# Moving four of sixteen heads of a score product from GpSimd to VectorE, and a division one step later

## What is computed

```python
att = jnp.einsum('bthd,btgd->bthg', q, k) / jnp.sqrt(jnp.float32(Dh))   # Dh = 8
att = jax.nn.softmax(att, axis=-1)
out = jnp.einsum('bthg,btgd->bthd', att, v)
...
x = x + _L0_attn_ref(xn, ...) + _L0_ffn_ref(xn, ...)     # top 2 of 8 experts
```

## Time and profile before

| | |
|---|---|
| median of 3 runs | 1330.55 us (1329.0 to 1339.67) |
| the profiled execution's own time | 1335.22 us |
| its span, first to last instruction | 1333.3 us |
| busy: TensorE, weight loads, VectorE, ScalarE, GpSimd | 1042.1, 879.2, 739.9, 583.7, 803.9 us |
| GpSimd's products L294 | 42, 188.8 us |
| GpSimd's scatters of results L498, both layers | 284, 283.3 us |
| score reduces L1157 | 21, 92.6 us |

### The profile page before, as it was taken

One profiled execution on the slowest core, in us unless ns is written; L12 is line 12 of the kernel. 1 busy time (PEld: TensorE's weight loads), 2 busy tenths in 40 slices (PEclk: granted clock), 3 DMA queues, 4 the chain that ended last, 5 costly groups with the idle time before them and its releaser, 6 DMA issues. The chain is left out here.

```text
span 1333.3 us, 19064 instructions
## 1 busy us (share of the span) xinstructions
PE 1042.1 (78%) x6498; PEld 879.2 (66%) x6498; DVE 739.9 (55%) x953; ACT 583.7 (44%) x1518; POOL 803.9 (60%) x669
## 2 busy tenths in 40 slices
PE   5553776788988898888714678898879999999995
PEld 4521333367777777777613577888868888888884
DVE  7755988998888898888697643211122200000007
ACT  1200111166676777767503673000006666666651
POOL 4065675568888888888875136566544544444444
PEclk9876886799999999999856888998979999999998
DMA  9912322335554555555281021698966867666649
GB/s 294 355 47 102 120 84 109 108 93 151 155 162 139 154 170 149 161 150 159 68 325 57 1 84 44 197 279 252 296 196 195 270 193 196 194 190 196 199 135 356
DMA packets 120245, 226.03 MB, mean 170 GB/s; under 512 B 16961, under 2 KB 80405, under 8 KB 118102
## 3 DMA queue, kind: packets, MB, share of 16 engines
q1 hardware_dynamic: 102164, 188.45, 46.1%
q0 software_dynamic: 17600, 35.71, 7.3%
q10 hardware_dynamic: 386, 0.66, 0.2%
HBM read 157.33 MB, written 67.42 MB: 169 GB/s over the span
## 5 line engine op out<-in xcount | busy, mean ns | idle before, releaser
L498 POOL DMA_INDIRECT y_tok<-FF,yidx x284 | 283.3, 997 | 205.9 <-ACT FF L586 142.6
L490 POOL DMA_INDIRECT sorted_x<-XN,idx x256 | 247.9, 968 | 140.1 <-issue 88.0
L810 PE MATMUL ps<-FF 128*128 128x128 f32 x2272 | 285.8, 280 | 0.0
L810 PEld LDWEIGHTS ps<-FF 128*128 128x128 f32 x2272 | 274.0, 197 | 15.6 <-issue 4.8
L797 PE MATMUL ps<-FF 128*128 128x256 f32 x1136 | 272.3, 383 | 0.0
L576 ACT ACTIVATE FF<-ps,FF 128x256 f32<-128x256 f32 x568 | 231.4, 473 | 36.8 <-PE ps L797 29.1
L797 PEld LDWEIGHTS ps<-FF 128*128 128x128 f32 x1136 | 206.9, 192 | 22.7
L294 POOL TENSOR_TENSOR BG<-TPB 128x2048 f32<-128x2048 f32 x42 | 188.8, 4519 | 30.0 <-ACT TPB L603 20.8
L838 PE MATMUL ps<-BG,cst 128*128 128x512 f32 x176 | 105.4, 767 | 57.8 <-DVE BG L1144 40.5
L1176 DVE TENSOR_TENSOR BG<-ps,TPB 128x1024 f32<-128x1024 f32 x128 | 147.3, 1212 | 0.0
L1187 DVE TENSOR_REDUCE BG<-BG 128x256 f32<-128x4096 f32 x32 | 141.0, 4406 | 0.0
(11 more groups left out here) (203 smaller groups left out, 1462.0 us busy)
## 6 DMA issues: line engine op xcount, KB each, us to landing
FF<-in_moe SPq DMA_DIRECT2D x142, 514.0 KB
TPB<-in_kpad SPq DMA_DIRECT2D x22, 1024.0 KB
sorted_x<-TPB SPq DMA_DIRECT2D x36, 520.0 KB, 5.4
FF<-sorted_x SPq DMA_DIRECT2D x142, 130.0 KB
BG<-y_tok SPq DMA_DIRECT2D x12, 1024.0 KB, 9.2
FF<-in_kpad SPq DMA_DIRECT2D x10, 1024.0 KB
y_tok<-FF,yidx POOLq DMA_INDIRECT x284
xt_d<-BG SPq DMA_DIRECT2D x16, 256.0 KB, 4.4
```

Source lines behind the costliest of these rows:

```text
L490: pool.indirect_dma_start(sorted_x[layer], bass.IndirectOffsetOnAxis(ap=idx[:, k, j:j + 1], axis=0), XN[:, j, :], None).then_inc(s_sc, 16)
L498: pool.indirect_dma_start(y_d[layer], bass.IndirectOffsetOnAxis(ap=yidx[:, G % 4, r:r + 1], axis=0), ys[:, G % 4, r * D:(r + 1) * D], None ...
L810: t = pe.matmul(psY[:, r * P:(r + 1) * P], hT[:, G % 2, m, r * P:(r + 1) * P], wc[:, G % 4, HID + m * D:HID + (m + 1) * D], start=False, s ...
```

## The change

In `scores(b)`, for `b` from 10 to 30, VectorE waits until q, k and v of pair `b + 1` are copied, and multiplies the last four heads of the second tile of pair `b + 1`. This stands behind the score reduce of pair `b` and ahead of its maximum. GpSimd's second half of a product shrinks from 16 heads to 12. The score reduce waits for both. The division (`by_sums`, formerly the end of `weighted`) of pairs 10 to 29 moves from the end of step `b + 1` into step `b + 2`, behind the score reduce and behind the new product, ahead of the maximum. Other pairs keep it in its old place.

```diff
+H_DVE = 4
...
-                    for t in range(2):
-                        qk_product(pool, b + 1, t).then_inc(s_pp, 1)
+                    qk_product(pool, b + 1, 0).then_inc(s_pp, 1)
+                    qk_product(pool, b + 1, 1, 0, H - H_DVE).then_inc(s_pp, 1)
...
+            mine, divided = {}, {}
+
             def scores(b):
...
                     dve.wait_ge(s_pp, 2 * (b - OWN) + 2)
+                    dve.wait_ge(s_v, mine[b])
                     link(dve.tensor_reduce(S[:, b % 2, :], prod[:, b % 2, :].rearrange("p (n d) -> p n d", d=DH),
                                            AX.X, ALU.add))
                     raw = S3
+                if OWN - 1 <= b < NPAIR - 1:
+                    dve.wait_ge(s_qkv, 2 * (b + 1) + 2)
+                    mine[b + 1] = mark(qk_product(dve, b + 1, 1, H - H_DVE, H_DVE))
+                if b > OWN:
+                    by_sums(b - 2)
                 wait(dve, s_sub, b)
                 link(dve.tensor_reduce(Mx, raw, AX.X, ALU.max))
...
                 reduced = mark(dve.tensor_reduce(O, prodv.rearrange("p (n g) -> p n g", g=H), AX.X, ALU.add))
-                dve.wait_ge(s_v, max(inverted, reduced))
+                divided[b] = max(inverted, reduced)
+                if not OWN - 1 <= b < NPAIR - 2:
+                    by_sums(b)
+
+            def by_sums(b):
+
+                dve.wait_ge(s_v, divided[b])
                 wait(dve, s_ot, b - 2)
                 dve.tensor_tensor(On[:, b % 3, :].rearrange("p (n e) -> p n e", e=DH), O.rearrange("p (n e) -> p n e", e=DH),
                                   Rc[:, :, None].to_broadcast([P, 2 * H, DH]), ALU.mult).then_inc(s_on, 1)
```

## The result

The changed kernel takes 1342.30 us in the median of 20 runs (1329.71 to 1352.03), the kernel before 1329.40 us in 20 runs beside it (1321.49 to 1339.67). The ratio is 1.0089, with a 95% interval of 1.0069 to 1.0110: about 12 us slower, where 2 us were forecast. The profiled execution took 1343.59 us, with a span of 1341.6. In the changed file the lines have moved by 2 to 16: the product is L296, the scatter L500, the copy of q, k, v L605, ScalarE's work on a finished tile L586 and L588; VectorE's score reduce is L1162, maximum L1171, subtraction L1172, `add_heads` L1177, division L1206.

The account below looks back on a forecast made before the run. GpSimd's loop of products, scatters and a wait for ScalarE's copy was taken as the bound. Start +1.4, nine two-pair stretches at +0.2, end -1.1 gave about +2 on the median 1330.55: 1333 us, range 1314 to 1345.

Parts of the forecast that it names:

- the new wait: VectorE waits for the next pair's copy before the maximum; even products start 2.50 us behind it, 2.41 more than before.
- rival B: Ring of four result buffers rules, ScalarE waits for landed first scatters; two pairs grow 1.3 us, 1345 us; chance 0.13.
- the sum per two pairs: GpSimd's loop over two pairs: -2.2 from its shorter halves, +2.41 from the later even start, +0.2 us.
- GpSimd's second half: GpSimd's product with 12 heads in place of 16: 1.1 us saved a pair, 2.2 for two.
- VectorE's new product: VectorE's product of 512 elements ahead of the maximum: taken as 0.61 us, upper end 0.69.
- Odd pairs unchanged: GpSimd's odd products start as before, behind the eight scatters, with 1.25 us of cover left.
- Start of the stretch: Pairs 10 to 12: GpSimd's product of pair 12 starts at 292.2 in place of 290.85, +1.4 us.
- End of the stretch: From the product of pair 30 on, everything comes 1.1 us earlier relative to that product's start.
- The copy: ScalarE's copy of q, k, v before an even product was taken as tied to the end of GpSimd's six scatters.
- rival A: Copy not tied to the scatters' end, time falls: 1320 us, chance 0.16, or 1297 us, chance 0.07.
- The two never meet: VectorE's new product and GpSimd's product of the same pair never overlap, since GpSimd's waits for the subtraction.
- Rival C: GpSimd's second half stays near 4.5 us despite fewer heads: +23 us, 1354 us; chance 0.05.

Follow-up runs that it names:

- experiments 3: Kernel before plus only VectorE's wait for the next pair's q, k, v copies ahead of the maximum; 1342.03 us, ratio 1.0093.
- experiment 8: Changed kernel with the division put back into its old place, ahead of the score reduce; 1334.48 us, ratio 1.0057 to the kernel before.
- experiment 5: Kernel before with the two scatters of each step's first tile moved between the halves of GpSimd's product; 1318.35 us, ratio 0.9950.
- experiment 12: Kernel before with each step's last tile scattered between the halves of GpSimd's next product; 1324.28 us, ratio 0.9985.
- experiment 2: Changed kernel reduced to the moved division: GpSimd multiplies all 16 heads, VectorE none, no wait for the copy; 1327.28 us, ratio 0.9989.
- experiment 6: Kernel of experiment 1 with the two scatters of each step's first tile moved between GpSimd's product halves; 1308.99 us, ratio 0.9866.
- experiment 1: Changed kernel with VectorE's four heads multiplied one step later, just ahead of their own score reduce; 1330.49 us, ratio 1.0032.

## Why the prediction came out as it did

The forecast was no change that can be told, 1333 us; 1342 lies inside its range, and the ratio of 1.0089 just inside its bound of 1%. The loop, the new wait and its price were read rightly. That the time stayed inside the range is in part luck: its upper end stood where it did for rival B. The step that failed is the sum per two pairs, +0.2 us, which measured +1.61, so that the loss is six times the 2 us forecast. (A slip besides: by its own terms the forecast's inner range should begin at 1333 - 11 = 1322, not 1324.)

- *GpSimd's second half*, -2.2 per two pairs: -2.16. Right.
- *VectorE's new product*, 0.61 us: 484.50 to 485.11. Right.
- *The new wait*, even products 2.50 us behind the copy: 2.60. Right, and experiments 3 and 8 show its parts: 1.65 for the wait with maximum and subtraction, 0.34 for the division.
- *Odd pairs unchanged*: right.
- *Start of the stretch*, +1.4: right. From the end of pair 11's copy, for which the first of the new waits waits, to the start of product 12 it took 18.00 us before (272.85 to 290.85) and 19.51 now (271.68 to 291.19). Counted from the start of the span product 12 is only 0.34 later, because this execution came to pair 11's copy 1.17 us earlier:

```profile
271.20 0.48 ACT L605 COPY TPB<-ps 128x384 f32<-128x384 f32 x1 [1.67 <-PE ps L855]
291.19 7.92 POOL L296 TENSOR_TENSOR BG<-TPB 128x2048 f32<-128x2048 f32 x2 [9.31 <-DVE BG L1172]
```

- *End of the stretch*, -1.1: product 30 starts 14.8 us later than before and the last scatter of layer 0 ends 13.4 later (681.70 against 668.30): -1.4. Right. From pair 11's copy to that scatter the change costs 14.6 us. The two profiled executions end only 8.3 us apart: besides the 1.17 us at the start, 5 us were made up behind that scatter, which the change does not touch, and why isn't shown.
- *The copy*, taken as fixed to the end of the six scatters: it came 0.78 us later. This is the first term that was missing. It did stay behind the last scatter (rival A fell), but its distance isn't fixed, and under another order of the scatters it ends ahead of them (experiment 5). Why the distance grew stays open.
- *"The two never meet"*: true of the two products. But VectorE's product and subtraction met GpSimd's scatters, in the run of eight, and each stretched one: +0.65 there, +0.46 for both runs, the second missing term. Before, the subtraction did so only at times: the scatter at 514.40 took 1.45 us.

Rival B named a time near to the measured one, but its sign did not come: ScalarE's stop for landed scatters is 1.34 us at 498.70, against 1.04, and did not grow by the 1 us that the prediction asked of it. From 270 to 690 us ScalarE's waits ahead of a finished tile are now these (those of the kernel before stand under experiment 12):

```profile
ACT yidx L586 <- remote: 47.2, 18, 3.6
...
ACT yidx L586 <- DMA y_tok<-FF,yidx: 15.1, 10, 2.1
```

The waits for landed scatters grew from 11.7 to 15.1 us, those without a named releaser from 23.8 to 47.2. Still, the copy kept its distance to the first of the eight scatters better than that to the last of the six: 28.48 us before and 28.64 after on the mean of the nine, against 1.89 and 2.68. So B's sum, +1.3 per two pairs, is nearer to the +1.61 than the forecast's, without the cause that it named. Rival C fell with the halves. The division cost the 0.34 that the prediction gave it in the chain (experiment 8), and nothing by itself (experiment 2).

## What to carry to other kernels

Before an engine is given work ahead of a result that others wait for, look at when its inputs come: a wait in that place was paid in full here, and it ate the whole gain of a lighter GpSimd. If the input is late, ask first why; reordering GpSimd's scatters made it early, and the same change then gained 1.2%. When an order is changed, look also at which instructions of two engines now meet: the division that took 0.42 us took 2.5 in experiment 5. And when a loop has been shortened, read its slowest repetitions and not only the typical one.

## What the runs showed of the hardware

- A scatter (an indirect DMA issued by GpSimd) that starts while VectorE runs an instruction with two SBUF inputs ends 0.83 to 0.87 us behind that instruction's end. This held for all 24 scatters of the changed kernel that started 0.2 us or more ahead of such an end (lengths 1.24 to 1.97 us, otherwise 0.96) and for all 24 of experiment 6. Four scatters that started within 0.03 us of the start of such an instruction were not stretched (two in the kernel before, two in experiment 2), nor was any that was already running (20 in the kernel before, 31 in experiment 6: at most 1.00 us). Beside VectorE's reduces over 4096 elements, which have one input, all 104 of the changed kernel took 0.95 to 1.00 us. The Trainium skill ("SBUF — State Buffer", section "Who interferes with whom") reports that such VectorE instructions didn't stall GpSimd's DMAs in a probe, with the reason marked as inferred; the rows here differ, and the measurement decides.
- During a long run of scatters TensorE's signals reach ScalarE late: in experiment 1 a product that ended at 511.30 by its row was taken up at 513.73. In the changed kernel ScalarE's long stops without a named releaser end 0.83 to 0.91 us behind the last of eight scatters (nine times) and 1.05 to 1.36 behind the last of six (eight times). By the trace's semaphore events each was ended by TensorE's signal, not by a landed scatter: for the stop that ends at 506.50 that signal came at 506.48, and the product's row ends at 501.62. The length of the run doesn't decide alone: the six scatters in a row of experiment 12 held hardly any. Rows of TensorE have modelled ends, so how much of this is the signal and how much the work isn't settled, nor is the cause.
